# A four-layer graph network on one core: dense products in three bf16 parts, register loads in halves, pair counts over two banks

## The reference

```
edge_index = stack([src, dst])
h = max(layernorm(x), 0);  x = x + L0(h, edges, weights)   # 2 graph convolutions with batch norm
h = max(layernorm(x), 0);  x = x + L1(h, edges, edge_attr) # attention, 4 heads
h = max(layernorm(x), 0);  x = x + L2(h, edges)            # attention, 8 heads
h = max(layernorm(x), 0);  x = x + L3(h, edges)            # 2 layers of the kind below

def layer(h, row, col, Wt, bt, Wg, bg):                    # L3, twice, relu behind each
    h = h @ Wt.T + bt
    deg = clip(segment_sum(ones, row), 1);  dinv = deg ** -0.5
    g = tanh(h[row] @ Wg + bg)
    msg = (g * dinv[row] * dinv[col])[:, None] * h[row]
    return segment_sum(msg, col) + h
```

## Time and profile before

| what | value |
|---|---|
| median of three runs | 3535.09 us (3529.31 to 3539.81) |
| the profiled execution: its own time | 3526.88 us |
| its span in the profile | 3525.0 us |
| mean granted clock of PE | 0.715 of full |
| busy: PE, PEld, DVE, ACT, POOL | 63%, 56%, 68%, 36%, 57% |
| first block pass, first product to the closing one | 3003.89 to 3239.06 us |
| second block pass | 3272.90 to 3508.48 us |

### The profile page before, as it was taken

The page is one execution under the profiler, slowest core; times in us unless marked ns, Lnnn a source line. Parts: engine busy times, 40 slices in busy tenths (PEclk is TensorE's granted clock), DMA queues, the critical chain, the costliest instruction groups (busy, mean ns, idle before and its releaser), DMA issues.

```text
span 3525.0 us, 60164 instructions
## 1 busy us (share of the span) xinstructions
PE 2205.9 (63%) x15246; PEld 1969.1 (56%) x15273; DVE 2399.7 (68%) x7660; ACT 1283.6 (36%) x3489; POOL 2004.9 (57%) x2076
## 2 busy tenths in 40 slices
PE   4992240566665567677556676545455455999998
PEld 3991230455554355555445575535455453998998
DVE  7997960777776669999726556575778777433434
ACT  4220020223332123333357767735777774000000
POOL 1777777777776477777267777716777770000000
PEclk9995555676666655555656556667777777999999
DMA  2210000111113123333333333224444441221222
GB/s 82 69 59 4 4 22 27 48 53 52 53 52 48 53 72 93 92 92 92 41 97 82 81 77 80 68 27 149 130 132 131 130 114 24 73 76 52 69 75 63
DMA packets 171637, 250.17 MB, mean 71 GB/s; under 512 B 52006, under 2 KB 120412, under 8 KB 171154
## 3 DMA queue, kind: packets, MB, share of 16 engines
q0 software_dynamic: 72704, 138.94, 16.2%
q1 hardware_dynamic: 94276, 96.20, 9.2%
q10 hardware_dynamic: 4430, 12.43, 1.0%
HBM read 217.00 MB, written 30.41 MB: 70 GB/s over the span
## 4 chain that ended last, share of the span: by engine, by line
POOL 48%; PE 21%; issue 18%; DVE 9%; DMA 2%; ACT 2%; DVEq 1%; POOLq 0%; ACTq 0%; SPq 0%
POOL arena L715 20%; POOL pool L715 17%; PE psum L1504 8%; POOL rec_dram L692 7%; PE psum L1500 5%; POOL ACC L715 3%; PE psum L1230 2%; DVE ACC L2336 1%; PE psum L1268 1%; DVE arena L2062 1%; ACT pool L816 1%; PE psum L1105 1%; DVE pool L2324 1%; DMA arena<-tab_dram,tblk 1%; DVE pool L1725 1%
## 5 line engine op out<-in xcount | busy, mean ns | idle before, releaser
L715 POOL DMA_INDIRECT arena<-tab_dram,tblk x832 | 796.6, 957 | 411.1 <-issue 250.8
L692 POOL DMA_INDIRECT rec_dram<-arena,ACC x400 | 396.1, 990 | 196.5 <-issue 118.9
L715 POOL DMA_INDIRECT pool<-tab_dram,arena x416 | 401.3, 965 | 131.4 <-issue 126.5
L1551 PE MATMUL psum<-pool 128*128 128x136 f32 (+1 forms) x1664 | 361.4, 398 | 82.8 <-DVE pool L2260 76.6
L1551 PEld LDWEIGHTS psum<-pool 128*128 128x128 f32 x1664 | 335.0, 289 | 94.9 <-issue 57.6
L1382 PE MATMUL psum<-pool 128*128 128x128 f32 x832 | 193.0, 426 | 294.6 <-DMA pool<-tab_dram,arena 206.9
L2116 DVE CAST pool<-pool 128x1024 f32<-128x1024 uint8 x264 | 182.4, 694 | 278.1 <-PE psum L1504 168.1
L2062 DVE TENSOR_SCALAR arena<-fwd,arena 128x128 bf16<-128x128 bf16 x2112 | 359.1, 287 | 0.8 <-PE psum L1424 0.8
L1382 PEld LDWEIGHTS psum<-pool 128*128 128x128 f32 x832 | 179.8, 328 | 299.0 <-DVE pool L2129 129.9
L715 POOL DMA_INDIRECT pool<-tab_dram,tblk x272 | 263.9, 970 | 125.5 <-issue 80.2
L857 ACT ACTIVATE arena<-psum,key 128x128 bf16<-128x128 f32 x416 | 146.4, 377 | 473.5 <-PE psum L1325 473.5
(11 more groups left out here) (373 smaller groups left out, 4891.7 us busy)
## 6 DMA issues: line engine op xcount, KB each, us to landing
pool<-items_dram SPq DMA_DIRECT2D x264, 128.0 KB, 2.1
pool<-dst_dram SPq DMA_DIRECT2D x104, 256.0 KB, 3.5
items_dram<-pool SPq DMA_DIRECT2D x132, 128.0 KB, 2.0
arena<-tab_dram,tblk POOLq DMA_INDIRECT x832
HN<-in_edge_attr_dram ACTq DMA_DIRECT2D x23, 500.0 KB
pool<-tab_dram,arena POOLq DMA_INDIRECT x416
rec_dram<-arena,ACC POOLq DMA_INDIRECT x400, 2.1
pool<-tab_dram,tblk POOLq DMA_INDIRECT x272
```

Of the source, the lines that this page charges most:

```text
L692: nc.gpsimd.indirect_dma_start(rec_dram, bass.IndirectOffsetOnAxis(ap=row_all[:, c:c + 1], axis=0), rec_all[:, c, :], None).then_inc(s_sca ...
L715: nc.gpsimd.indirect_dma_start(to[:, j, :], None, tab_dram[k], bass.IndirectOffsetOnAxis(ap=idx[:, G * g + j:G * g + j + 1], axis=0)).then ...
L1551: last_ = nc.tensor.matmul(bank[j // 3][:, (j % 3) * ww:(j % 3 + 1) * ww], OHF[:, half, j, :], weighed[k][:, half, j, :], start=True, stop ...
```

## The change

In the block passes the dense items' weights become bf16, and each dense product becomes three: the table's float32 numbers are cut into three parts of which each is exact in bf16. The upper half of a float32's bits is itself a bf16; `high` is a view on these upper halves (every second 16-bit number, a step of 4 bytes). DVE writes `rest` = table - high(table) and `tail` = rest - high(rest) behind each chunk of the table, and PE adds item x high(table), item x high(rest) and item x high(tail). The 16 registers are loaded as two times 8, the first in the midst of the group's first dense pack, the second behind its last. The other 416 items a pass stay float32. At the start, ACT copies the counts of two batches with each operation (two neighbouring banks, 32 by 200), and the edge_features steps 0 and 1 stand behind the counts.

```diff
+        bite16 = [b[:, 0:PACK * P // 2].bitcast(BF16) for b in bite32]
+        rest = big[:, NP:2 * NP]
+        tail = arena[:, 3 * NB * D + NB * 8:3 * NB * D + NB * 8 + NP]
+        def high(ap):
+            halves = ap.bitcast(BF16)
+            (step, count) = halves.ap[-1]
+            return bass.AP(halves.tensor, halves.offset + 1, [*halves.ap[:-1], [2 * step, count // 2]])
...
             def pair_counts(c):
-                act.wait_ge(s_both, c + 1)
-                of = bank[4 + c % 4][:, :].rearrange("p (g k) -> p g k", k=P)
+                n = min(2, BATCHES - c)
+                act.wait_ge(s_both, c + n)
+                of = psum[:, 512 * (4 + c % 4):512 * (4 + c % 4 + n)].rearrange("p (g k) -> p g k", k=P)
                 for j in range(4):
                     lo, hi = KEYS * j, KEYS * (j + 1)
-                    nc.scalar.activation(upto[lo:hi, :, 4 * c:4 * c + 4].rearrange("p s g -> p g s"), of[lo:hi, :, lo:lo + NB],
+                    nc.scalar.activation(upto[lo:hi, :, 4 * c:4 * (c + n)].rearrange("p s g -> p g s"), of[lo:hi, :, lo:lo + NB],
                                          ACT.Copy).then_inc(s_upto, 1)
...
-            for c in range(BATCHES):
+            for c in range(0, BATCHES, 2):
                 pair_counts(c)
-                if c == 6:
-                    edge_features(0)
-                elif c == 14:
-                    edge_features(1)
             turned_keys(0)
+            edge_features(0)
             for b in range(BATCHES):
                 if b + 1 < BATCHES:
                     turned_keys(b + 1)
+                if b == 0:
+                    edge_features(1)
                 if b + 2 < BATCHES:
                     edge_features(b + 2)
...
-            def item_regs(q):
+            def item_regs(q, half):
...
-                    where[0:1, 2 * G * q:2 * G * (q + 1)], engines=[pe.engine], min_val=0, max_val=NB - 1,
+                    where[0:1, G * (2 * q + half):G * (2 * q + half + 1)], engines=[pe.engine], min_val=0, max_val=NB - 1,
...
+                ahead = []
                 for m, b in bites(k):
-                    vals = item_regs(b - firsts) if b >= firsts else None
+                    vals = ahead if b >= firsts else None
                     pe.wait_ge(s_cast, m + 1)
                     for j in range(PACK):
-                        item, w = bite32[m % HELD][:, P * j:P * (j + 1)], PACK * b + j
+                        if not vals and j == 4 and b == firsts * q_of(b) // GROUPS:
+                            ahead.append(item_regs(q_of(b), 0))
+                        item, w = (bite32 if vals else bite16)[m % HELD][:, P * j:P * (j + 1)], PACK * b + j
...
-                            last = nc.tensor.matmul(psum[:, d * P:(d + 1) * P], item, table[:, of * AW:of * AW + D], start=False, stop=False)
+                            for part in (table[:, of * AW:of * AW + D], rest[:, of * D:(of + 1) * D], tail[:, of * D:(of + 1) * D]):
+                                last = nc.tensor.matmul(psum[:, d * P:(d + 1) * P], item, high(part), start=False, stop=False)
                     last.then_inc(s_part, 1)
+                    if vals:
+                        ahead = []
+                    elif b + 1 == firsts * (q_of(b) + 1) // GROUPS:
+                        ahead.append(item_regs(q_of(b), 1))
...
                     dve.wait_ge(s_taken, before(stage, c, MADE) + 1)
+                    whole = TAB[:, 4 * c:4 * c + n, 0:D]
+                    link(v.tensor_tensor(feature_chunk(rest, c, n), whole, high(whole), ALU.subtract))
+                    link(v.tensor_tensor(feature_chunk(tail, c, n), feature_chunk(rest, c, n), high(feature_chunk(rest, c, n)), ALU.subtract))
                     dve.sem_inc(s_table, 1)
...
-                    v.tensor_copy(bite32[m % HELD], bite8[m % LONG]).then_inc(s_cast, 1)
+                    v.tensor_copy((bite16 if b < FIRSTS // PACK else bite32)[m % HELD], bite8[m % LONG]).then_inc(s_cast, 1)
```

More of the change, by code:

```diff
@@ L24 @@
 BATCHES = COLS // BATCH
+COUNTED_ALL = 4 * ((BATCHES + 1) // 2)
 KEYS = 32
@@ L1194, in pair_counts @@
                 if c >= 4:
-                    pe.wait_ge(s_upto, 4 * (c - 3))
+                    pe.wait_ge(s_upto, 4 * ((c - 4) // 2 + 1))
                 for q in range(4):
@@ L1217, in turned_keys @@
                     pe.wait_ge(s_tot, 1)
-                    pe.wait_ge(s_upto, 4 * BATCHES)
+                    pe.wait_ge(s_upto, COUNTED_ALL)
                 for q in range(4):
@@ L1478, in turn_sums, with q_of @@
                 last.then_inc(s_itemp, 1)
-            def item_regs(q):
+            def item_regs(q, half):
                 _, vals = nc.values_load_multi_w_load_instructions(
-                    where[0:1, 2 * G * q:2 * G * (q + 1)], engines=[pe.engine], min_val=0, max_val=NB - 1,
+                    where[0:1, G * (2 * q + half):G * (2 * q + half + 1)], engines=[pe.engine], min_val=0, max_val=NB - 1,
                     skip_runtime_bounds_check_because="the table holds block numbers of at most NB - 1")
                 return vals
+            def q_of(b):
+                return next(q for q in range(GROUPS) if b < FIRSTS // PACK * (q + 1) // GROUPS)
             def block_pass(k):
@@ L1493, in block_pass @@
                 pe.wait_ge(s_table, CHUNKS * k)
+                ahead = []
                 for m, b in bites(k):
-                    vals = item_regs(b - firsts) if b >= firsts else None
+                    vals = ahead if b >= firsts else None
                     pe.wait_ge(s_cast, m + 1)
                     for j in range(PACK):
-                        item, w = bite32[m % HELD][:, P * j:P * (j + 1)], PACK * b + j
+                        if not vals and j == 4 and b == firsts * q_of(b) // GROUPS:
+                            ahead.append(item_regs(q_of(b), 0))
+                        item, w = (bite32 if vals else bite16)[m % HELD][:, P * j:P * (j + 1)], PACK * b + j
                         if vals:
-                            last = nc.tensor.matmul(psum[:, bass.ds(vals[G + j] * P, P)], item, table[:, bass.ds(vals[j] * AW, D)],
+                            last = nc.tensor.matmul(psum[:, bass.ds(vals[1][j] * P, P)], item, table[:, bass.ds(vals[0][j] * AW, D)],
                                                     start=False, stop=False)
@@ L1670, in _ @@
             link(v.memset(tcount[:, 3, :], 0.0))
-            dve.wait_ge(s_upto, 4 * BATCHES)
+            dve.wait_ge(s_upto, COUNTED_ALL)
             link(v.tensor_reduce(tot[:, :], upto, AX, ALU.add))
@@ L2111, in block_pass @@
                 dve.sem_inc(s_free, 1)
-                for m, _ in bites(k):
+                for m, b in bites(k):
                     dve.wait_ge(s_bite[m // 2 % 4], bite_loads(m))
```

## The result

The changed kernel takes 3494.16 us, median of 4 runs (3490.67 to 3497.5), beside 3532.41 us (3529.31 to 3539.81, 4 runs) for the kernel before: a ratio of 0.9888, 95% interval 0.987 to 0.9905. The forecast was 3497 us and a change of -38.4; measured is -38.2. The profiled execution has a span of 3495.7 us against 3525.0 before, so 29.3 less: it was the slowest of its four, and gave back 5 us in the record and gather stages between 590 and 2983 us, which the change does not touch.

What follows compares the result with a forecast made beforehand. PE was taken as the bound of the block passes, its sequencer next. -37.2 (passes) + 9.3 (tables) - 10.5 (start) = -38.4 us took the median from 3535.1 to 3497 us; range 3480 to 3512, chance 0.60.

Steps and rivals of the forecast that it cites:

- The passes: Both block passes: bf16 dense products, partly held by PE's sequencer, bring each to 217 us, together -37.2 us.
- a queue of some 16 pairs: PE's sequencer in the block passes: gets at most 16 load-and-product pairs ahead, 0.90 us of bf16 work.
- The bound of 200 us a pass: Block passes: lower limit if the sequencer cost nothing, 200 us a pass, -71 us for both.
- the slow start: Start of each block pass: PE's first three microseconds at half clock add 1.6 us.
- The two-pack group: Block-pass groups with two dense packs: 2.69 us dense, 1.99 second kind, 0.04 more; 4.72 us each, 28 of them.
- The strided operand: Dense products, rival: operand with 4-byte step read at half rate, 0.112 us a pair, 3654 us in all; chance 0.11.
- Load and product overlap: Dense products, rival: no overlap in a long stream, 0.081 us a pair, pass 245 us, 3554 in all; chance 0.05.
- the sequencer costs nothing: Block passes, rival: sequencer works further ahead than read, so PE alone sets the pace, 3463 us in all; chance 0.12.
- the two slower rivals: Dense products: half-rate operand reads (3654 us) or no overlap of load and product (3554 us); together chance 0.16.
- The start: Ahead of the first scatter: ACT's doubled counts let DVE sum at 47.1 instead of 57.64 us, -10.5 us.
- The moved scores: Start: edge_features(0) and (1) moved behind the counts were put at zero cost, with 10 us left.
- The tables: Stages 6 and 7: two more DVE operations behind each chunk, +3.1 and +6.2, together +9.3 us.

Runs made afterwards that it cites:

- one-load kernel: Changed kernel with a group's 16 registers loaded in one instruction just ahead of their products, as before: 3537.53 us, ratio 1.0023 to the kernel before.
- two kernels without loads: Changed kernel with constant block numbers (no register loads or arithmetic): 3471.55 us; changed kernel with registers loaded once a pass, arithmetic kept: 3469.32 us.
- two-part kernels: Changed kernel with tail left out of the sums: 3437.75 us; with tail not made either and both loads early: 4680.17 us, ratio 0.977 to the kernel before.
- run 14: Not a label: an instruction executed 14 times, in the better-order kernel with the table's third part made by POOL instead of DVE: 3485.33 us, ratio 0.9869.

## Why the prediction was right

**The passes.** Forecast 217 us, measured 216.5; -37.2 forecast, -37.8 measured. The mechanism is the one named: a queue of some 16 pairs (17 by the count above), and register loads that must fit in it. Groups were forecast at 3.46 and 4.72 us and take 3.48 and 4.71. The one-load kernel (239 us, not 216), the two kernels without loads (205.5 to 205.8) and the two-part kernels (190.5 and 181.8, where PE alone would give 181 and 170.5) each exclude that PE alone sets the pace. The bound of 200 us a pass was too low: PE's own work is 205.8, since a pair takes 0.0573 and not 0.056 (2.4 us), a change of kind 0.055 (2.9 us), which the sum did not have, and the slow start 2.5 us and not 1.6. The two-pack group came out right because that term stood in it unseen in place of a somewhat smaller stop: 4.59 is PE's own, the sequencer adds 0.12, where I had 4.48 and 0.24. The sum has one more slip: it counts 28 groups at 4.72, though the last one holds two dense products and takes 3.5. These 1.2 us too many and the slow start (2.2 us with the loads in place, put at 1.6) partly cancel, so 217 is nearer than its terms are.

**The rivals.** The strided operand costs 0.0014 us a pair, not 0.051 to 0.056. Load and product overlap in the long stream too: 48 pairs at 0.057 each in every group with two dense packs. The 81 ns of the Trainium skill (TensorE: Matmul & The Clock Gate, section Back-to-back issue gap) is not what this stream shows: the trace disagrees, with 57 ns. That strides within a 16-byte line are free (the Trainium skill, SBUF — State Buffer, section Door 1: The DMA port swizzle) now has a run beside it, and it nearly agrees: 1.4 ns a pair. That the sequencer costs nothing is excluded by the runs above. The prediction says that all but the two slower rivals lie in 3480 to 3512; its own 3463 for this one does not.

**The start.** -10.5 forecast, -10.8 measured alone. ACT's doubled operation takes 0.517 us, not 0.45, but four of them repeat every 2.41 us and 0.25 of that is a wait for PE's next counts, which follow DVE's keys (2.4 us a pair of batches); so the size did not matter. The moved scores held nothing up.

**The tables** are where a size was off: +9.3 forecast, +15.4 in the profiled execution. Stage 6 was put at +3.1 and took +5.9. 1.3 of that is the clearing of the sums, 2.8 us at half clock where before it had been 1.5 at full; the rest is DVE, which falls behind from the first chunk (a chunk 2.56 us, not 2.33: 0.22 of waits on its own last operation, which my sum of 0.85 + 0.08 + 1.40 left out). Stage 7 was put at +6.2 and took +9.5: 6.5 is DVE's end, near the forecast, and 3.1 is PE at half clock ahead of it. In the windows of PE in stage 7, after and before (before at the same part of the stage):

```profile
3230.00:3243.00 13.00, 12.37 (x43) 8.50 (x40) 4.95 (x9) 2.82 (x7) 0.00 (x0) 0.50 0.00 0
```
```profile
3250.00:3262.00 12.00, 9.37 (x52) 6.14 (x51) 4.79 (x9) 4.08 (x9) 0.00 (x0) 0.87 0.01 1
```

It comes and goes: with three parts and DVE alone, stage 7 took 39.1, 40.1, 40.3, 40.3, 40.6, 41.3, 41.9, 42.0, 42.8 and 43.4 us in ten profiled executions, and 33.8 in both without the parts. With stage 6 at +5.9, the tables cost 11 to 15 us, not 9.3; the prediction put the clock's part at nothing. That the total came out within 1 us is partly luck: -37.8, -10.8 and +11 to +15 add up to -33 to -38, and the medians, uncertain by some 6 us here, say -38.2.

## What to carry to other kernels

A faster product can turn a hidden cost of the sequencer into the bound: count, per group, register loads (0.59 us for eight) and address arithmetic (0.25 us a product) beside PE's work, and ask how many pairs are in hand when the load starts. Put the loads where cheap work follows them, and keep products of one type together. And read starts, not idle times: PE showed 1 us of waits where the sequencer cost it 21 in two passes.

## What the runs showed of the hardware

- PE's sequencer gets 17 pairs of load and product ahead of PE and no further, be they bf16 (0.97 us of work) or float32 (1.9 us): so it is at every register load behind a full dense pack in the kernel with one load, and in 100 of 102 in the kernel before.
- A run of float32 pairs between bf16 pairs costs 0.055 us beyond the pairs' own times. This order was new; before, all products of a block pass were float32.
- PE stayed at 1.2 GHz through 7.9 us of unbroken one-row products of 512 columns, and through 13 us of stage 7 in which it was busy for 12.4; what would have raised it is not shown.
- One arithmetic instruction more in POOL's program, run 14 times near the end, goes with some 8 ns more for each indirect transfer, in one pair of kernels. The cause is not known.
- An operation of DVE of 1 or 4 columns on two operands in on-chip memory (L1975) that starts beside POOL's 128x512 one ends when POOL's ends: it lasts 0.38 to 1.02 us instead of 0.15.
